# The bias of the folded weights: added on VectorE behind the transposes instead of on GpSimd at once

## The reference, cut to what matters

```
y  = cond(x)                      # per sequence one 64x64 matrix, chosen by a token
x1 = x + attention(y)             # 32 query heads, 8 key heads, width 128, causal ALiBi, rms-normed q and k
h  = x1 @ W2.T + b2 + scale * (x1 @ A.T) @ B.T      # A and B chosen per sequence
out = x1 + h @ Wbase.T + b_base + 0.5 * fourier(h @ enc.T, masked coefs)
```

## Time and profile before

| what | value |
|---|---|
| median of 3 runs | 2450.15 us (2449.34 to 2452.37) |
| the profiled execution's own time | 2451.36 us |
| its span (first to last instruction) | 2449.5 us |
| mean granted TensorE clock | 0.992 |
| TensorE matmuls | 2389.1 us busy, 98% |
| VectorE | 1717.5 us busy, 70% |
| ScalarE | 1322.7 us busy, 54% |
| GpSimd | 244.6 us busy, 10% |
| DMA | 316.13 MB, mean 129 GB/s |

### The profile page before, as it was taken

The page is one execution under the profiler, slowest core; times in us unless marked ns, Lnnn a source line. Parts: engine busy times, 40 slices in busy tenths (PEclk is TensorE's granted clock), DMA queues, the critical chain, the costliest instruction groups (busy, mean ns, idle before and its releaser), DMA issues.

```text
span 2449.5 us, 32848 instructions
## 1 busy us (share of the span) xinstructions
PE 2389.1 (98%) x11676; PEld 1981.6 (81%) x11676; DVE 1717.5 (70%) x2766; ACT 1322.7 (54%) x3265; POOL 244.6 (10%) x272
## 2 busy tenths in 40 slices
PE   7989999999999999999999999999999999999998
PEld 5877788888788888888788888888788888888787
DVE  5547968786845777777854777777774686868682
ACT  3235646465624656566633666665643575756560
POOL 0101000001021101010011101010010101000101
PEclk8989999999999999999999999999999999999999
DMA  5356453632632242424344242423254242424250
GB/s 207 121 192 238 160 201 138 222 122 86 204 116 96 78 146 75 150 71 137 112 159 145 69 155 69 155 70 103 87 191 138 69 138 87 135 89 131 68 198 35
DMA packets 88437, 316.13 MB, mean 129 GB/s; under 512 B 12716, under 2 KB 13228, under 8 KB 87124
## 3 DMA queue, kind: packets, MB, share of 16 engines
q1 hardware_dynamic: 70292, 247.14, 29.8%
q10 hardware_dynamic: 10944, 37.54, 4.1%
q0 software_dynamic: 7040, 29.36, 3.3%
HBM read 282.54 MB, written 31.46 MB: 128 GB/s over the span
## 4 chain that ended last, share of the span: by engine, by line
PE 92%; DVE 4%; issue 1%; DMA 1%; ACT 1%; ACTq 0%; POOL 0%; DVEq 0%; POOLq 0%
PE main L950 78%; PE pv_bank L1134 3%; PE qt_bank L1099 3%; PE s_bank L1115 2%; PE s_bank L1116 2%; PE pt_bank L1123 1%; PE pt_bank L950 1%; DVE ring L1399 1%; PE s_bank L950 1%; PE qt_bank L950 1%; DMA sums<-in_wo 1%; DVE acc L1402 0%; DMA t_scratch<-sums 0%; ACT prob L1295 0%; PE qt_bank L1038 0%
## 5 line engine op out<-in xcount | busy, mean ns | idle before, releaser
L950 PE MATMUL main<-ring,act_hi 128*128 128x512 f32 x3584 | 1151.5, 402 | 0.0
L950 PEld LDWEIGHTS main<-ring,act_hi 128*128 128x128 f32 x3584 | 643.1, 189 | 111.4
L950 PE MATMUL main<-ring,act_lo 128*128 128x512 f32 x1792 | 703.3, 392 | 0.0
L950 PE MATMUL main<-ring,lefts 128*128 128x512 f32 x2688 | 626.2, 391 | 12.3 <-ACT main L1145 12.3
L1399 DVE TENSOR_TENSOR ring<-raw,ring 128x1024 fp32r<-128x1024 f32 x448 | 548.7, 1228 | 71.1 <-ACT ring L1145 69.1
L950 PEld LDWEIGHTS main<-ring,lefts 128*128 128x128 f32 x2688 | 501.1, 188 | 117.5 <-ACT main L1145 14.9
L1145 ACT ACTIVATE ring<-raw 128x1024 fp32r<-128x1024 f32 x448 | 472.2, 1056 | 218.4 <-PE main L950 213.6
L950 PEld LDWEIGHTS main<-ring,act_lo 128*128 128x128 f32 x1792 | 337.6, 188 | 74.6
L1720 POOL TENSOR_TENSOR rstd<-mean,half 128x4 f32<-128x4 f32 (+1 forms) x192 | 174.5, 909 | 1619.3 <-DVE mean L1509 1619.3
L1295 ACT ACTIVATE prob<-score,peak 128x64 f32<-128x64 f32 x512 | 136.6, 337 | 172.1 <-DVE peak L1564 172.1
L1267 ACT ACTIVATE sq<-main 128x128 f32<-128x128 f32 x640 | 168.1, 276 | 62.6 <-PE main L950 60.2
(11 more groups left out here) (141 smaller groups left out, 2347.9 us busy)
## 6 DMA issues: line engine op xcount, KB each, us to landing
raw<-in_wq SPq DMA_DIRECT2D x128, 512.0 KB, 4.1
raw<-t_scratch SPq DMA_DIRECT2D x128, 512.0 KB, 3.3
raw<-in_wo SPq DMA_DIRECT2D x96, 512.0 KB, 3.3
raw<-in_wkv SPq DMA_DIRECT2D x64, 512.0 KB, 3.7
sums<-in_wo ACTq DMA_DIRECT2D x32, 512.0 KB, 6.8
t_scratch<-sums ACTq DMA_DIRECT2D x32, 512.0 KB, 3.7
raw<-f_scratch SPq DMA_DIRECT2D x32, 512.0 KB, 4.8
acc<-in_x POOLq DMA_DIRECT2D x16, 512.0 KB, 3.6
```

The costliest lines, as they stand in the source:

```text
L950: mm = eng.matmul(bank, a, b, start=start and n == 0 and m == 0, stop=stop and n == len(terms) - 1 and m == 2, skip_group_check=further)
```

## The change

The stage `biased_x` moves from GpSimd's program to VectorE's, with the same two waits and the same operands. In the order list it no longer stands directly behind the transposes of its tile: it is due 3.2 quarters later.

```diff
-          x1=2.2, low=4.0, out=0.6,
+          x1=2.2, bias=3.2, low=4.0, out=0.6,
@@ transpose_x1
             self.act("x1", blk, t, i)
-        self.add("biased_x", blk, t)
+        self.later(AT["bias"], lambda: self.add("biased_x", blk, t))
@@ block.vector
+                elif stage == "biased_x":
+                    blk, t = key
+                    w.wait_ge("x1_t", blk, t, 1)
+                    w.wait_ge("bias_add", 1)
+                    add(acc[:, t, :], acc[:, t, :], bias_eff[:, :], stage)
@@ block.gpsimd
-                elif stage == "biased_x":
-                    blk, t = key
-                    w.wait_ge("x1_t", blk, t, 1)
-                    w.wait_ge("bias_add", 1)
-                    eng.tensor_tensor(acc[:, t, :], acc[:, t, :], bias_eff[:, :], ALU.add).then_inc(done[stage], 1)
```

## The result

The changed kernel takes 2453.6 us (median of 22 runs, 2451.01 to 2457.11); the kernel before, run beside it, 2450.33 us (22 runs, 2447.54 to 2456.85). The ratio is 1.0014 with a 95% interval of 1.0007 to 1.0020: slower by 1.7 to 4.9 us, by the medians 3.3. The forecast was 2454.5, 0.18% slower; the change is within the 0.2% that the text before called no measurable change, and 22 runs a side tell it from nothing.

The account below looks back on a forecast made before the run. TensorE, busy 98% of the span, bounds the kernel. Terms of -0.24 and +1.34 make +1.10 us a block, +4.4 in all, from a median of 2450.15 to 2454.5 us, 0.18% slower; range 2449.0 to 2458.0.

Parts of the forecast that it names:

- What bounds: Whole kernel: TensorE, busy 98% of the span, is the bound; only microseconds in which it stands still count.
- What is removed, -0.24 us a block: GpSimd sums stretching a VectorE subtraction to 1.91 us: without them the first low-rank product starts 0.24 us sooner.
- Where the sums land: VectorE's queue: sums A and B stand ahead of the low parts ending the chain, which has 0.16 us slack.
- Price of a sum, 1.14 us: Each sum on VectorE costs the start-to-start pitch of a 128x1024 operation, 1.14 us.
- Sums C and D cost nothing: Sums of a block's third and fourth tiles fall behind the second low-rank split, before 4.21 us of VectorE idle time.
- Term +1.34 us a block: Second low-rank product: its last low part ends 1.50 us later, less 0.16 slack; TensorE stands still 1.34 us more.
- Sum +4.4 us: Whole kernel: -0.24 and +1.34 make +1.10 us a block, +4.4 us in all.
- The rule that a VectorE operation waits for an empty pipeline: Skill's alternative price: each chain sum would cost its full 1.22 us, 0.6 more in all, 2455.1; rows contradict it.
- B: Rival: VectorE has room, TensorE does not stall, only the stretching's end remains; -1.0 us, 2449.2; chance 0.12.
- C: Rival: the longer stall lets TensorE's clock fall, 6.9 us in all, 2461.4; chance 0.06.
- D: Rival: sums or what is queued behind cost 0.2 to 0.7 us a block beyond pitch; 2455.3 to 2457.3; chance 0.15.
- The far price ends, 0.60 and 1.83: Lowest and highest pitch considered for a VectorE sum, in us, giving times of 2450.2 and 2460.1.

Follow-up runs that it names:

- e7: Changed kernel with the low-rank product due 4.9 instead of 4.0 quarters behind the product; 2446.53 us, 0.9986 of the kernel before.
- e6: Kernel before with the GpSimd sum cut to 8 of 1024 columns; 2448.91 us, 1.0000 of the kernel before.
- e1: Changed kernel with all four VectorE sums due 7.5 instead of 3.2 quarters behind the transposes; 2449.79 us, 0.9995 of the kernel before.
- e9: Changed kernel with VectorE sums due earlier, 2.9 (A, C) and 0.9 (B, D) quarters behind their transposes; 2451.37 us, 1.0003 of the kernel before.
- e4: Changed kernel with only sum B moved, due 7.5 instead of 3.2 quarters behind its transposes; 2448.81 us, 0.9992 of the kernel before.
- e10: Changed kernel with each sum over 512 of 1024 columns, at the same place; 2450.41 us, 1.0001 of the kernel before.
- e5: Changed kernel with each sum made twice in a row on VectorE at the same place; 2467.93 us, 1.0084 of the kernel before.

## Why the prediction was right

- **What bounds.** Right. In this stretch only TensorE's waits for `act_lo` changed, and the periods follow from them to 0.1 us a block, that of e7 to 0.15.
- **What is removed, -0.24 us a block.** Right: e6 has -0.25, e1 -0.29, e9 -0.25; the first wait fell from 0.51 to 0.29 us. e1 and e9 carry all four sums on VectorE beside it.
- **Where the sums land.** Right. The queue order was read off the due times: 8.2 comes ahead of 8.6 and 8.8, 10.2 ahead of 10.6 and 10.8. Moving them off the chain (e1, e9), one of them (e4), or giving the chain room (e7) removes the loss.
- **Price of a sum, 1.14 us.** Right where sums stand alone: e10's half width and the starts 685.54 to 686.67 agree. The second of two sums of the same tile in a row costs 1.26 (e5).
- **Sums C and D cost nothing.** Right: e1 has all four sums behind the splits, and its period (567.34) is not above that of e6 (567.38), which has none on VectorE.
- **Term +1.34 us a block.** 1.05 + 0.24 = 1.29 by the period; in block 0 it is 21.42 - 20.33 + 0.24 = 1.33, 20.33 being 694.60 - 674.27 before. The visible second wait is 0.83 us, below the 1.0 to 1.3 that the prediction gave as its sign; this sign failed, and the term did not. From start to start the wait is 1.21 - 0.23 = 0.98. Tile D's transposes add 0.24 (the prediction had about 0.3, inside the same term): they run from 689.15 to the matmul at 690.16, before from 688.80 to 689.59, and start 0.02 later behind the first product. The first matmul behind the wait adds 0.08, together 1.30.
- **Sum +4.4 us.** 4.2 by the periods, 3.3 by the medians (1.7 to 4.9).
- **The rule that a VectorE operation waits for an empty pipeline** (the Trainium skill, VectorE: DVE Perf Modes, "The DRAIN you can't avoid"): the rows of 685.54 and 686.67 show 1.13 us from start to start for an operation of 1.22, so the time followed the pitch. The prediction left out that the same section lets an operation that is not held start earlier, which agrees with these rows. e5's dependent sums stand 1.26 us apart, further than their duration.
- **Rivals.** B fell because of the order, as argued; its time is what e1 and e9 reach by moving the sums, 567.34 and 567.38. C did not happen: clock 1.00 over 4 us behind each second wait of the changed kernel; in e5, with 1.3 us more of this wait and another of 1.13 us ahead of it, it fell in two blocks of four. D did not happen: sums and what is queued behind them kept pitches of 1.13 to 1.14 and 0.60. The far price ends, 0.60 and 1.83, did not come up for the full sums.

## What to carry to other kernels

Idle time of an in-order engine can be used only by what stands ahead of the wait that ends it. To move an operation, write down the queue it joins with start-to-start pitches, find the last entry that the bounding engine waits for, and compare its slack (here 0.16 us) with the pitches put ahead of it; the engine's load decided nothing, and that VectorE makes the sum in 1.22 us where GpSimd takes 2.40 did not help, since the sum costs only through the pitch that it puts on the chain. Where run times scatter by more than the effect, a distance between two repeated events in one trace measures it: here to about 0.1 us, where medians of a dozen runs could not.

## What the runs showed of the hardware

- A VectorE subtraction of two SBUF operands beside a GpSimd sum of two SBUF operands took 1.91 and 1.65 us in place of 1.22; with the GpSimd sum cut to 8 columns, and over before the subtraction starts, it took 1.23 (e6). VectorE operations with a PSUM operand kept 0.68 us beside the sum. The Trainium skill, SBUF — State Buffer, "Who interferes with whom", says that a VectorE instruction with two SBUF inputs contends with a GpSimd instruction that reads SBUF. The trace agrees: the first subtraction overlaps the sum by 0.82 us and took 0.69 more.
- The granted clock fell behind a wait of 2.08 us in one block of e5 (0.57 over 4 us, at 1264.3) and of 2.10 us in another, and stayed at 1.00 behind waits of 2.08 and 2.09 us in the two others, with the same instructions in front. The length of the wait did not decide it elsewhere either: at the start of block 0, behind TensorE's wait for scores, it fell after 2.10 us in e1_late (0.69 over 4 us) and stayed at 1.00 after 2.78 us in e10_half:
```profile
334.01:338.01 4.00, 4.00 (x17) 3.33 (x18) 3.37 (x7) 1.06 (x4) 1.01 (x1) 0.69 0.98 391
```
```profile
335.04:339.04 4.00, 4.00 (x23) 3.44 (x24) 3.37 (x7) 1.06 (x4) 1.01 (x1) 1.00 0.98 391
```
Behind the four waits of 0.83 us of the changed kernel it did not fall.
